# A two-layer gated cross-attention kernel: the split of the row maxima moves from VectorE to GpSimd

## The chip, the core and the metric

The kernel runs on one core of one Trainium2 chip. The metric is the device time of one execution in microseconds (us), of which the median of three runs is taken. A core has TensorE (matrix products), VectorE, ScalarE and GpSimd (elementwise work), each with its own queue that runs in order; they wait for one another by semaphores. SyncE's queue issues most of the transfers.

## The reference

Four batches of 512 rows with 128 channels pass two layers, each a gated cross-attention and a gated feed-forward part:

```python
x = x + tanh(g_xattn[0]) * attention0(layernorm(x), ctx, ctx)     # 16 heads of 8, 154 keys
x = x + tanh(g_ffn[0])   * quantised_mlp(layernorm(x))
x = x + tanh(g_xattn[1]) * attention1(layernorm(x), ctx, ctx)     # causal mask
x = x + tanh(g_ffn[1])   * gated_scan(layernorm(x))               # a recurrence over the four batches
# attention: softmax(q k^T / sqrt(8)) v, then a linear layer
```

The softmax needs the maximum of each row of scores to stay in range.

## The kernel before

**Row maxima first.** For each layer and batch (`n = 4 * layer + batch`) the kernel computes the scores twice. In the first pass TensorE (`scores_for_top`) writes scores with the 512 queries across partitions, some three heads at a time, to the three banks `ps_top`, and VectorE (`take_top`, L1333) reduces each to the negated row maximum in `nm`, 4 tiles of queries by 16 heads, so 64 numbers in each of 128 partitions. `split_top` makes two parts of type fp32r of `nm` in the tile `nms`: a high part, which is `nm` copied to fp32r (L1344), and a low part, `nm` less the high part (L1346). `turn_top` on TensorE (L967) transposes them into `ps_misc`, `copy_top` on ScalarE (L763) copies that to `nmT`, and two transfers on SyncE's queue (`tops`, L446) lay it as two more rows under the queries in `Q4`. In the second pass (`scores`, L985 and L991) each product so gives the score with its maximum taken off; ScalarE (`exps`, L772) takes the exponential, and TensorE (`weigh`, L1017) multiplies it with the values.

**The order of work.** Each engine's instructions stand in an order written out by hand. A loop runs over the layer, over `i` from -1 to 4, and over 20 slots. In iteration `i` the second pass of batch `i` (20 tiles, one a slot), the first pass of batch `i + 1` (slots 0 to 12), and the end of batch `i - 1` (division, output product, residual, statistics of the next norm) run side by side. `PE_PLAN`, `ACT_PLAN` and `DVE_PLAN` say at which slot the other pieces stand: VectorE's split of batch `i + 1` at slot 13, `turn_top` and `copy_top` at slot 14, the statistics for the norm `post` of batch `i - 1` at slot 9 and its transposes at slot 16 (18 in layer 1). The first reductions of batch `i + 2` stand in slots 17 to 19, behind `turn_top` in TensorE's order, and write `nm` again.

**GpSimd's order** has no slots. In an iteration it runs, in this order: the norm `pre` of a later batch, its block-diagonal keys (`diagonal`, L521) and the low part of its queries (`q_low`, L614), for `i` = -1 and 1 only; in layer 1 the causal masks `past(i, 0)` to `past(i, 2)` (L620), each of which waits for four exponentials, the third for that of tile 11; the norm `post` of batch `i - 1` (`normed`: L626, the power L628, L636 and four instructions `xn` of L643); in layer 1 `past(i, 3)`, which waits for tile 15; and `biased(i + 1)` (four additions, L604), which `residual` needs in the next iteration. `biased(0, 0)` stands at the end of iteration -1.

Of the kernel before, what the change touches and what calls it, by code (L numbers as in the profile page):

```python
# [7 lines left out]
F32 = mybir.dt.float32  # L8
# [3 lines left out]
ALU = mybir.AluOpType  # L12
# [4 lines left out]
B, T, C = 4, 512, 128  # L17
# [3 lines left out]
G, J = 4, 4  # L21
# [68 lines left out]
def units_before(n):  # L90

    return sum(len(UNITS[m // B]) for m in range(n))
# [109 lines left out]
def program(nc, x, w, wkr, ctxT, tailT, wffn, cols, rows, consts, masks, out):  # L202
    with ExitStack() as ctx:
        def sb(name, shape, dt=F32):
            return ctx.enter_context(nc.sbuf_tensor("sb_" + name, shape, dt))
# [4 lines left out]
        def sem(name):  # L210
            return ctx.enter_context(nc.semaphore(name))
# [44 lines left out]
        nm = sb("nm", [P, TT, H])  # L256
        nms = sb("nms", [P, TT, 2, J, G], F32R)
# [91 lines left out]
        top_r, top_red = sem("top_r"), sem("top_red")  # L349
        nmh_r, nms_r, nmT_r = sem("nmh_r"), sem("nms_r"), sem("nmT_r")  # L350
# [117 lines left out]
        def _(pool):  # L468
# [17 lines left out]
            def clear_rest():  # L486

                pool.wait_ge(kd0_r, 1)
                pool.memset(Q4[2][:, :, :].bitcast(F32), 0.0).then_inc(q4_clear, 1)
                pool.memset(Kd[2][:, :, :, :].bitcast(F32), 0.0).then_inc(kd_clear, 1)  # L490
                pool.memset(nil[:, :], 0.0).then_inc(nil_r, 1)
# [49 lines left out]
            def biases():  # L541

                pool.wait_ge(rows_in, 16)
                pool.wait_ge(gates, 1)
                for n in range(2):
                    pool.tensor_scalar(bvt[:, n, :], rows_sb[:, RV + n, :], own[:, 0:1], 1.0, ALU.mult, ALU.mult)\
                        .then_inc(bias_r, 1)
                for n in range(2):
                    pool.tensor_scalar(bog[:, n, :], rows_sb[:, RO + n, :], tg[:, n:n + 1], 1.0, ALU.mult, ALU.mult)\
                        .then_inc(bias_r, 1)  # L550

            def frames():

                pool.memset(KT[:, :, :, :].bitcast(F32), 0.0).then_inc(zero_r, 1)
                pool.wait_ge(zero_r, 3)
                pool.wait_ge(ones_r, 1)
                pool.wait_ge(small_in, 32)
                pool.wait_ge(rows_in, 16)
                for j in range(J):
                    c = 16 * (j % 2) + D  # L560
                    for b in range(B):
                        ins = pool.memset(V4[:, b, :, j, c:c + D], 1.0)
                    link(ins)
                    q = slice(32 * j, 32 * j + 32)
                    on = ones[q, :].rearrange("p (b g d) -> p b g d", b=B, g=G)
                    link(pool.tensor_scalar(VT[q, :, :, 16 * j + D:16 * j + 2 * D], on, own[q, 0:1], 1.0,
                                            ALU.mult, ALU.mult))
# [26 lines left out]
            def biased(layer, b):  # L594
                n = B * layer + b
                if n >= 2:
                    pool.wait_ge(res_r, n - 1)
                if layer == 1:
                    pool.wait_ge(x2_r, b + 1)
                else:  # L600
                    pool.wait_ge(x_in[b], 16)
                pool.wait_ge(bias_r, 4)
                for t in range(TT):
                    ins = pool.tensor_tensor(xg[:, n % 2, t, :], xr[:, TT * b + t, :], bog[:, layer, :], ALU.add)  # L604
                ins.then_inc(xg_r, 1)

            def q_low(layer, b):

                n = B * layer + b
                pool.wait_ge(qh_r, n + 1)  # L610
                pool.wait_ge(qf_r, QLOW_ON_POOL.index((layer, b)) + 1)
                if n >= 2:
                    pool.wait_ge(*q_landed(n - 2))
                pool.tensor_tensor(ql[:, n % 2, :], qf[:, :], qh[:, n % 2, :].bitcast(F32), ALU.subtract).then_inc(ql_r, 1)  # L614

            def past(b, r):

                k = TILES * (B + b) + 4 * r
                pool.wait_ge(exp_r, k + 4)
                pool.affine_select(pr[:, k % PRING:k % PRING + 4, 0:P], pr[:, k % PRING:k % PRING + 4, 0:P],  # L620
                                   [[0, 4], [1, P]], ALU.is_ge, 0.0, base=0, channel_multiplier=-1).then_inc(past_r, 1)

            def root(k):

                pool.wait_ge(mv_r, k + 1)
                pool.tensor_scalar(var[:, k % 4, :], mv[:, k % 4, :, 1], EPS, 1.0, ALU.add, ALU.mult).then_inc(var_r, 1)  # L626
                pool.wait_ge(var_r, k + 1)
                pool.tensor_tensor(rstd[:, k % 4, :], var[:, k % 4, :], half[:, :], ALU.pow).then_inc(rstd_r, 1)  # L628

            def normed(kind, layer, b):  # L630

                k = norm_no[kind, layer, b]
                root(k)
                if (kind, layer, b) in NORM_ON_DVE:
                    return
                pool.tensor_scalar(nmean[:, k % 4, :], mv[:, k % 4, :, 0], -1.0, 1.0, ALU.mult, ALU.mult).then_inc(nmean_r, 1)  # L636
                nmeans[0] += 1
                pool.wait_ge(nmean_r, nmeans[0])
                pool.wait_ge(rstd_r, k + 1)
                if B * layer + b > 0:  # L640
                    pool.wait_ge(xnT_r, norm_no[kind, (B * layer + b - 1) // B, (b - 1) % B] + 1)
                for t in range(TT):
                    ins = pool.tensor_scalar(xn[:, kind == "post", t, :], xr[:, TT * b + t, :], nmean[:, k % 4, t:t + 1],  # L643
                                             rstd[:, k % 4, t:t + 1], ALU.add, ALU.mult)
                ins.then_inc(xn_r, 1)
# [3 lines left out]
            for layer in range(2):  # L649
                normed("pre", layer, 0)  # L650
                if layer == 0:
                    pool.wait_ge(xn_r, 1)
                    pool.memset(Kd[1][:, :, :, :].bitcast(F32), 0.0).then_inc(kd_clear, 1)
                    pool.memset(V4[:, :, :, :, :], 0.0).then_inc(zero_r, 1)
                    pool.memset(VT[:, :, :, :], 0.0).then_inc(zero_r, 1)
                normed("pre", layer, 1)
                if layer == 0:
                    clear_rest()
                    normed("pre", 0, 2)
                    frames()  # L660
                    biases()
                    values(0)
                    q_low(0, 2)
                    tail_keys(0)
                else:
                    clear_late()
                for i in range(-1, B + 1):
                    masked = layer == 1 and 0 <= i < B
                    if i == -1 or 0 < i < B - 2:
                        b = max(i, 0) + 2  # L670
                        if i > 0:
                            normed("pre", layer, b)
                        if masked:
                            past(i, 0)
                        diagonal(layer, b)
                        if (layer, b) != (0, 2):
                            q_low(layer, b)
                    elif masked:
                        past(i, 0)
                    if masked:  # L680
                        past(i, 1)
                        past(i, 2)
                    if 0 <= i - 1 < B:
                        normed("post", layer, i - 1)
                    if masked:
                        past(i, 3)
                    if 0 <= i + 1 < B:
                        biased(layer, i + 1)
                if layer == 0:
                    pool.wait_ge(xq_r, B)  # L690
                    diagonal(1, 0)
                    values(1)
                    tail_keys(1)
                    clear_early()
# [530 lines left out]
        def _(dve):  # L1225
# [109 lines left out]
                                  AX.X, ALU.max, negate=True).then_inc(top_red, 1)  # L1335

            def split_top(layer, b):
                n = B * layer + b
                dve.wait_ge(top_red, units_before(n + 1))
                src = nm[:, :, :].rearrange("p t (g j) -> p t j g", g=G)  # L1340
                part = [nms[:, :, a, :, :] for a in range(2)]
                if n > 0:
                    dve.wait_ge(nmT_r, n)
                dve.tensor_copy(part[0], src).then_inc(nmh_r, 1)  # L1344
                dve.wait_ge(nmh_r, n + 1)
                dve.tensor_tensor(part[1], src, part[0].bitcast(F32), ALU.subtract).then_inc(nms_r, 1)  # L1346
# [337 lines left out]
```

## Time and profile before

| | |
|---|---|
| runs | 343.42, 342.97, 343.03 us, median 343.03 |
| profiled execution, first to last instruction (span) | 341.2 us; its own time isn't listed apart from the three runs |
| TensorE busy | 279.0 us |
| VectorE busy | 252.5 us |
| ScalarE busy | 192.6 us |
| GpSimd busy | 136.7 us |
| the 8 splits on VectorE | median 0.316 + 0.326 us each |

The profile is of one execution. PE is TensorE, DVE VectorE, ACT ScalarE, POOL GpSimd, SP SyncE; L967 is line 967 of the kernel. The end of a matmul is modelled. The number behind x counts the instructions of a group.

### The profile page before, as it was taken

The page shows a single profiled execution, that of the slowest core. Times are in us where ns is not written, and L with a number is a line of the kernel's source. Part 1 is how long each engine was busy: PE and PEld are TensorE (multiplying, and loading weights), DVE is VectorE, ACT ScalarE, POOL GpSimd, SP SyncE. Part 2 cuts the span into 40 slices and gives each one's busy share as a digit, 9 for nine tenths or more (in the row PEclk, how much of TensorE's full clock was granted, in tenths as well). Part 3 has the DMA queues.
Part 4 walks back from the last instruction along what each step waited for, and adds up shares of the span by engine and source line. Part 5 has one row for each costly group of instructions (what it writes and reads, how often), then busy time and mean ns, then how long its engine had stood idle before and what let it go on. Part 6 is the DMA issues. An engine that isn't in the chain of part 4 may idle for free. (4 is left out here: it accounts for less than half of the span.)

```text
span 341.2 us, 4468 instructions
## 1 busy us (share of the span) xinstructions
PE 279.0 (82%) x1424; PEld 160.7 (47%) x1424; DVE 252.5 (74%) x538; ACT 192.6 (56%) x303; POOL 136.7 (40%) x274
## 2 busy tenths in 40 slices
PE   0889899899989779985007888899998998999994
PEld 0558544455434345331005776664654654444462
DVE  5699875877996388889989977986596693441834
ACT  1673367556476746779589632446656446665232
POOL 6669893750050411870002059921386207131100
PEclk9999999999999999997556999999999999999998
DMA  7930100010000000000000002220001000000004
GB/s 204 336 146 3 69 32 10 27 73 10 1 8 3 0 0 2 1 0 0 1 0 0 2 0 92 94 100 2 10 25 76 8 0 10 1 0 3 0 1 123
DMA packets 9687, 12.55 MB, mean 37 GB/s; under 512 B 896, under 2 KB 5376, under 8 KB 9664
## 3 DMA queue, kind: packets, MB, share of 16 engines
q1 hardware_dynamic: 9232, 11.80, 9.7%
q10 hardware_dynamic: 432, 0.47, 0.7%
q8 instruction: 11, 0.18, 0.2%
q14 instruction: 12, 0.10, 0.1%
HBM read 4.27 MB, written 1.05 MB: 16 GB/s over the span
## 5 line engine op out<-in xcount | busy, mean ns | idle before, releaser
L1333 DVE TENSOR_REDUCE sb_nm<-ps_top 128x3 f32<-128x462 f32 (+2 forms) x168 | 96.0, 626 | 26.6 <-PE ps_top L953 13.9
L772 ACT ACTIVATE sb_pr<-ps_score 128x512 f32<-128x512 f32 (+1 forms) x148 | 82.3, 583 | 58.8 <-PE ps_score L985 49.2
L953 PE MATMUL ps_top<-sb_Kd,sb_Q 128*128 128x462 f32 (+3 forms) x240 | 69.7, 349 | 4.7 <-DVE sb_nm L1333 2.4
L985 PE MATMUL ps_score<-sb_Q,sb_Kd 128*128 128x512 f32 x119 | 54.4, 467 | 1.3 <-ACT sb_pr L772 1.0
L953 PEld LDWEIGHTS ps_top<-sb_Kd,sb_Q 128*128 128x128 f32 x240 | 42.6, 188 | 18.1 <-DVE sb_nm L1333 11.9
L626 POOL TENSOR_SCALAR sb_var<-sb_mv 128x4 f32<-128x4 f32 x16 | 4.7, 291 | 83.3 <-DVE sb_mv L1296 82.9
L985 PEld LDWEIGHTS ps_score<-sb_Q,sb_Kd 128*128 128x128 f32 x119 | 22.2, 188 | 31.6 <-ACT sb_pr L772 23.4
L1017 PE MATMUL ps_pv<-sb_pr,sb_V 128*32 128x512 f32 x256 | 34.1, 605 | 0.0
L620 POOL TENSOR_SCALAR_AFFINE_SELECT sb_pr<-sb_pr 128x512 f32<-128x512 f32 x16 | 10.6, 661 | 46.4 <-ACT sb_pr L772 46.4
L1353 DVE STREAM_TRANSPOSE sb_oq<-ps_pv 128x512 f32<-128x512 f32 x16 | 10.8, 700 | 12.4 <-PE ps_pv L1017 12.3
L643 POOL TENSOR_SCALAR sb_xn<-sb_xr,sb_nmean,sb_rstd 128x128 f32<-128x128 f32 x44 | 19.3, 453 | 1.2
L628 POOL TENSOR_TENSOR sb_rstd<-sb_var,sb_half 128x4 f32<-128x4 f32 x16 | 17.7, 1106 | 1.3
L521 POOL CAST sb_Kd<-sb_K 32x616 fp32r<-32x616 f32 x20 | 14.1, 703 | 8.5 <-DVE sb_K L1244 7.4
L1017 PE MATMUL ps_pv<-sb_pr,sb_VT 128*32 128x512 f32 (+1 forms) x128 | 14.9, 550 | 0.9 <-ACT sb_pr L772 0.9
L1102 PE MATMUL ps_top<-sb_wfT 128*128 128x256 f32 x30 | 9.5, 472 | 7.2 <-DVE sb_amax L1470 6.4
L991 PE MATMUL ps_score<-sb_Q,sb_KT 128*128 128x384 f32 (+1 forms) x29 | 12.9, 454 | 2.7 <-ACT sb_pr L772 2.7
L1293 DVE BATCH_NORM_STATS2 sb_stat<-sb_xr 128x6 f32<-128x128 f32 x64 | 13.9, 280 | 1.4 <-DMA sb_xr<-x 1.2
L497 POOL MEMSET sb_Q<- 128x2048 f32 x1 | 1.8, 1804 | 32.6 <-DVE sb_amax L1470 32.6
L930 PE MATMUL ps_misc<-sb_consts,sb_xn 128*128 128x128 f32 x64 | 10.4, 287 | 5.1 <-POOL sb_xn L643 2.3
L1195 PE MATMUL ps_top<-sb_front,sb_wfT 128*128 128x512 f32 x22 | 12.1, 682 | 2.7 <-ACT sb_uf L830 2.2
L1084 PE MATMUL ps_misc<-sb_consts,sb_amx 128*128 128x128 f32 x8 | 2.5, 400 | 14.2 <-DVE sb_amx L1403 14.2
L604 POOL TENSOR_TENSOR sb_xg<-sb_xr,sb_bog 128x128 f32<-128x128 f32 x32 | 13.6, 457 | 0.1
(180 smaller groups left out, 556.5 us busy)
## 6 DMA issues: line engine op xcount, KB each, us to landing
sb_Q<-sb_qh SPq DMA_DIRECT2D x16, 256.0 KB, 2.3
sb_Q<-sb_ql SPq DMA_DIRECT2D x8, 256.0 KB, 3.3
sb_xr<-x SPq DMA_DIRECT2D x4, 256.0 KB, 7.7
out<-sb_xr SPq DMA_DIRECT2D x4, 256.0 KB, 2.5
sb_wsb<-w SPq DMA_DIRECT2D x1, 704.0 KB, 9.0
sb_wf<-wffn SPq DMA_DIRECT2D x1, 576.0 KB, 8.6
sb_wkr<-wkr SPq DMA_DIRECT2D x2, 256.0 KB, 7.1
sb_Q<-sb_nmT SPq DMA_DIRECT2D x16, 32.0 KB
```

The lines of the kernel that those rows point to most:

```text
L521: ins = pool.tensor_copy(Kd[n % 3][q, :, j, :], K4[q, :, b, :])
L604: ins = pool.tensor_tensor(xg[:, n % 2, t, :], xr[:, TT * b + t, :], bog[:, layer, :], ALU.add)
L628: pool.tensor_tensor(rstd[:, k % 4, :], var[:, k % 4, :], half[:, :], ALU.pow).then_inc(rstd_r, 1)
L643: ins = pool.tensor_scalar(xn[:, kind == "post", t, :], xr[:, TT * b + t, :], nmean[:, k % 4, t:t + 1], rstd[:, k % 4, t:t + 1], ALU.add, ...
L772: act.activation(pr[:, k % PRING, q0:T], score_bank(B * layer + b, t)[:, q0:T], ACT.Exp, scale=SCALE).then_inc(exp_r, 1)
L953: ins = pe.matmul(cols[:, c0:c1, :], Q4[n % 3][:, g, P * qt:P * qt + P], Kd[n % 3][:, g, j:j + c1 - c0, 0:keys], start=True, stop=not mask ...
L985: ins = pe.matmul(ps[:, :], Kd[n % 3][:, g, j, 0:P], Q4[n % 3][:, g, :], start=True, stop=True, skip_group_check=True)
L991: ins = pe.matmul(ps[:, q0:T], KT[:, b, t - H, :], Q4[n % 3][:, t - H, q0:T], start=True, stop=(layer == 0), skip_group_check=True)
L1017: ins = pe.matmul(acc[32 * g:32 * g + 32, q0:T], lhs, pr[:, (TILES * n + t) % PRING, q0:T], start=(r in (0, 2)), stop=(r >= 4), skip_group ...
L1195: pe.matmul(fbank[t % FRING][:, :], wfT[:, 3 * (t // 12) + m, :], xq[:, c, :], start=True, stop=True).then_inc(fmm, 1)
L1293: ins = dve.bn_stats(stat6[:, k % 4, t, :], xr[:, TT * b + t, :])
L1333: dve.tensor_reduce(nm[:, :, :].rearrange("p t h -> p (t h)")[:, f0:f0 + heads], top[k % MRING][:, 0:keys * heads].rearrange("p (h k) -> p ...
```

## The change

The two instructions of `split_top` for batches 1, 2 and 3 of each layer run on GpSimd; VectorE keeps batch 0 of each layer. The semaphores stay the same. On GpSimd the call stands behind `normed("post", layer, i - 1)` and ahead of `past(i, 3)` and `biased(layer, i + 1)`.

```diff
+            def split_top(layer, b):
+
+                n = B * layer + b
+                pool.wait_ge(top_red, units_before(n + 1))
+                src = nm[:, :, :].rearrange("p t (g j) -> p t j g", g=G)
+                part = [nms[:, :, a, :, :] for a in range(2)]
+                pool.wait_ge(nmT_r, n)
+                pool.tensor_copy(part[0], src).then_inc(nmh_r, 1)
+                pool.wait_ge(nmh_r, n + 1)
+                pool.tensor_tensor(part[1], src, part[0].bitcast(F32), ALU.subtract).then_inc(nms_r, 1)
+
...
                     if 0 <= i - 1 < B:
                         normed("post", layer, i - 1)
+                    if 0 < i + 1 < B:
+                        split_top(layer, i + 1)
                     if masked:
                         past(i, 3)
                     if 0 <= i + 1 < B:
...
             def split_top(layer, b):
+                if b > 0:
+                    return
                 n = B * layer + b
                 dve.wait_ge(top_red, units_before(n + 1))
```

## Rows read from the trace of the kernel before

**Rows 1.** The page: busy time of each engine; granted clock in 40 slices
```profile
PE 279.0 (82%) x1424; PEld 160.7 (47%) x1424; DVE 252.5 (74%) x538; ACT 192.6 (56%) x303; POOL 136.7 (40%) x274
...
PEclk9999999999999999997556999999999999999998
```
**Rows 2.** The tile `nms`: duration in ns (min/median/max), first and last start
```profile
L1344 DVE CAST sb_nms<-sb_nm x8: 217/316/664, 34.7 to 284.2; 128x64 fp32r<-128x64 f32 x8
L1346 DVE TENSOR_TENSOR sb_nms<-sb_nm,sb_nms x8: 264/326/409, 35.0 to 284.5; 128x64 fp32r<-128x64 f32 x8
```
**Rows 3.** Timeline, layer 0, batch 1: start us, duration us, engine, line
```profile
49.70 3.36 POOL L604 TENSOR_TENSOR sb_xg<-sb_xr,sb_bog 128x128 f32<-128x128 f32 x8
50.68 0.38 DVE L1346 TENSOR_TENSOR sb_nms<-sb_nm,sb_nms 128x64 fp32r<-128x64 f32 x1
51.12 0.61 PE L967 MATMUL ps_misc<-sb_consts,sb_nms 128*32 128x128 f32 x4
```
**Rows 4.** Timeline, layer 0, batch 2
```profile
74.17 0.41 DVE L1346 TENSOR_TENSOR sb_nms<-sb_nm,sb_nms 128x64 fp32r<-128x64 f32 x1
74.63 0.61 PE L967 MATMUL ps_misc<-sb_consts,sb_nms 128*32 128x128 f32 x4
74.89 1.71 POOL L604 TENSOR_TENSOR sb_xg<-sb_xr,sb_bog 128x128 f32<-128x128 f32 x4
```
**Rows 5.** Timeline, layer 1, batch 1
```profile
236.43 0.64 POOL L620 TENSOR_SCALAR_AFFINE_SELECT sb_pr<-sb_pr 128x512 f32<-128x512 f32 x1 [3.86 <-ACT sb_pr L772]
237.44 0.27 DVE L1346 TENSOR_TENSOR sb_nms<-sb_nm,sb_nms 128x64 fp32r<-128x64 f32 x1
238.32 0.61 PE L967 MATMUL ps_misc<-sb_consts,sb_nms 128*32 128x128 f32 x4
```
**Rows 6.** Timeline, layer 1, batch 2; in brackets idle time before, and its releaser
```profile
259.28 0.64 POOL L620 TENSOR_SCALAR_AFFINE_SELECT sb_pr<-sb_pr 128x512 f32<-128x512 f32 x1 [2.56 <-ACT sb_pr L772]
...
260.29 1.03 POOL L628 TENSOR_TENSOR sb_rstd<-sb_var,sb_half 128x4 f32<-128x4 f32 x1
261.40 0.19 POOL L636 TENSOR_SCALAR sb_nmean<-sb_mv 128x4 f32<-128x4 f32 x1
...
261.54 0.26 DVE L1346 TENSOR_TENSOR sb_nms<-sb_nm,sb_nms 128x64 fp32r<-128x64 f32 x1
261.70 1.75 POOL L643 TENSOR_SCALAR sb_xn<-sb_xr,sb_nmean,sb_rstd 128x128 f32<-128x128 f32 x4
...
261.86 0.61 PE L967 MATMUL ps_misc<-sb_consts,sb_nms 128*32 128x128 f32 x4 [0.25 <-DVE sb_nms L1346]
...
264.68 1.44 DVE L1333 TENSOR_REDUCE sb_nm<-ps_top 128x4 f32<-128x512 f32 x2 [2.88 <-PE ps_top L957]
```
**Rows 7.** GpSimd: two groups by shape (busy us, mean ns), one line (min/median/max)
```profile
L604 POOL TENSOR_TENSOR sb_xg<-sb_xr,sb_bog 128x128 f32<-128x128 f32 x32 | 13.6, 457 | 0.1
L614 POOL TENSOR_TENSOR sb_ql<-sb_qf,sb_qh 128x512 fp32r<-128x512 f32 x4 | 5.1, 1277 | 3.3 <-ACT sb_qf L755 3.1
L534 POOL CAST sb_KT<-sb_K x8: 601/612/1232, 43.9 to 151.2; 32x512 fp32r<-32x512 f32 x8
```
**Rows 8.** TensorE's timeline; then stretches of 1 us, PEclk third from last
```profile
154.57 3.62 PE L1195 MATMUL ps_top<-sb_front,sb_wfT 128*128 128x512 f32 x4 [2.22 <-ACT sb_uf L830]
158.52 1.13 PE L1195 MATMUL ps_pv<-sb_front,sb_wfT 128*128 128x512 f32 x2 [0.33 <-ACT sb_uf L830]
...
222.06 0.61 PE L967 MATMUL ps_misc<-sb_consts,sb_nms 128*32 128x128 f32 x4 [1.57 <-DVE sb_nms L1346]
...
154.00:155.00 1.00, 0.43 (x1) 0.35 (x2) 1.00 (x1) 1.00 (x4) 0.00 (x0) 0.88 0.00 0
155.00:156.00 1.00, 1.00 (x2) 0.34 (x1) 1.00 (x2) 1.00 (x2) 0.00 (x0) 0.50 0.00 0
...
158.00:159.00 1.00, 0.67 (x2) 0.30 (x2) 0.96 (x2) 1.00 (x3) 0.00 (x0) 0.91 0.00 0
...
161.00:162.00 1.00, 0.00 (x0) 0.00 (x0) 1.00 (x3) 1.00 (x3) 0.00 (x0) 0.80 0.00 0
```

## The prediction

> **What bounds the kernel now.** I read the page's busy times first [rows 1]: TensorE is busy 82% of the span, VectorE 74%, GpSimd 40%. The average says that GpSimd has room for more; it doesn't say whether the room is where the split stands. So next the view of the tile that holds the two parts [rows 2]: eight CASTs and eight subtractions on VectorE, 0.32 and 0.33 us by the median. Who needs them is TensorE alone: `turn_top` stands in its queue right behind the scores of slot 14 and waits for `nms_r`; behind it in the same queue are the scores of tiles 15 to 19, and behind `copy_top` on ScalarE are their exponentials. So the question at each batch is one comparison of times: when do the parts land, and when does TensorE come to them? For that I read the timeline around each of the six splits that move [rows 3 to 6], with GpSimd's queue beside it.
>
> In layer 0 TensorE starts the four transposes 0.05 to 0.06 us after VectorE's subtraction ends: at 51.12 us after 51.06 [rows 3], at 74.63 after 74.58 [rows 4]. TensorE is waiting for the parts there already, by a little. In layer 1 the transposes start at 261.86 after 261.80, with TensorE idle 0.25 us before them [rows 6]. Only for batch 1 of layer 1 do they start well behind the parts, at 238.32 after 237.71 [rows 5]: TensorE had the weighing of round 2 to finish. So at five of six places the split ends the wait of the engine that has the most work, and any lateness is passed on whole.
>
> **The change, part by part.** What goes: six CASTs and six subtractions on VectorE. Worth nothing, I find: behind the split VectorE has nothing that could start sooner. In layer 1 its next reduction waits until 264.68, 2.88 us idle, for scores that TensorE issues behind the transposes [rows 6]; in layer 0 the next is the maximum of the normed rows, which waits for GpSimd's `xn`. That is the cover; without it six splits of 0.64 us would be 3.9 us [rows 2].
>
> What comes: the same two instructions on GpSimd, 64 elements in each of 128 partitions, with a wait between them. The trace has no such instruction there, so I work from its neighbours. A subtraction or addition took 457 ns at 128 elements and 1277 ns at 512 [rows 7]: 2.14 ns for one more element, so 0.32 us at 64. A CAST took 612 ns at 512 elements by the median [rows 7], and the instruction with 4 elements that writes `nmean` 0.19 to 0.20 us [rows 6]: 0.81 ns for one more, so 0.25 us at 64. The hand-over of one GpSimd instruction's result to the next is 0.08 us (261.32 to 261.40) [rows 6]. Together 0.65 us. From below each instruction costs at least those 0.20 us, so 0.48 for the split; from above each costs at most the 457 ns of one with 128 elements and two tensors, so 0.99. I take 0.65, since 64 elements lie between these sizes, and keep 0.48 and 0.99 for the range. From the end of the subtraction to TensorE's start I add the 0.05 us that VectorE's takes.
>
> The size of the instruction is the lesser part. The greater is where the split stands in GpSimd's queue, which runs in order: behind `normed("post", layer, i - 1)` and, in layer 1, behind `past(i, 2)`.
>
> Layer 0, batch 1: in front of it stands `biased(0, 0)`, the first four of the eight additions that begin at 49.70 [rows 3]; the row shows no idle time ahead of them, so the engine is not free earlier. Four take 1.7 us [rows 4], and the next instruction starts at 51.38. Parts at 52.03, TensorE at 52.08 in place of 51.12: 0.96 late. What moves behind the split is `biased(0, 1)`, which nobody needs before the residual of the next iteration.
>
> Layer 0, batch 2: `normed("post", 0, 0)` holds GpSimd until its next instruction starts at 74.89 [rows 4]. Parts at 75.54, TensorE at 75.59 in place of 74.63: 0.96 late. Batch 3 repeats this row by row (0.96 too). So 2.9 us for layer 0.
>
> Layer 1, batch 1: no `post` yet. GpSimd is idle after `past(0, 2)` ends at 237.07, and VectorE's split began some 0.25 us ahead of 237.44 [rows 5]. The parts would land at about 237.9, or at 238.2 by the upper bound, and TensorE comes at 238.32. No cost; the cover is 0.4 us.
>
> Layer 1, batch 2: `past(1, 2)` starts at 259.28, since it waits for the exponentials of tile 11; only then come the root, the mean and four `xn` of `normed("post", 1, 0)`, from 260.0 to 263.45 [rows 6]. The split starts at 263.40, as consecutive instructions overlap by 0.05. Parts at 264.05, TensorE at 264.10 in place of 261.86: 2.24 late. Batch 3 repeats it, again 2.24. So 4.5 us for layer 1. `past(i, 3)` and `biased(i + 1)` are now behind the split, but they wait for exponentials that come later by the same 2.24, so they cost nothing more.
>
> Stalls: 3 x 0.96 + 0 + 2 x 2.24 = 7.4 us. All later work of the iteration, on ScalarE, VectorE and the queue of the two DMAs of `nmT`, starts from these transposes, and I find no wait of TensorE behind them that ends on something that isn't late as well. So nothing is given back.
>
> **The clock.** The two stalls of layer 1 are longer than they look: TensorE already idles 0.25 us there, so each is a gap of 2.5 us. The trace has one gap of 2.22 us, before 154.57; the granted clock then fell from full (2.4 GHz) to half (1.2 GHz) at about 154.8 and was back at about 158.2, and the four matmuls in it took 3.62 us, 0.9 each. It fell a second time at about 161.6, when TensorE had been idle since 159.65. A gap of 1.57 us, before 222.06, brought no fall: the line of the page with the granted clock in 40 slices of 8.5 us shows full speed there [rows 1, 8]. So gaps like those of layer 0 (about 1 us) are safe, and each of the two in layer 1 may bring a fall. At half clock from 154.8 to 158.2, 3.4 us of matmul time do 1.7 us of work; after the transposes TensorE still has one short wait, so I take 1.6 us for a fall. The trace has two falls for gaps of this size and none for smaller ones, but the clock fell 2.4 us after TensorE's stop in one and 2.0 us after it in the other, so the length of the gap isn't all that decides, so I give each gap a chance of 0.55: none falls 0.2, one 0.5, both 0.3. One fall is the likeliest: +1.6.
>
> Sum: the median of the runs is 343.0, 1.8 above the profiled span of 341.2, and I add to the median as the parts around the span don't change. 343.0 + 7.4 + 1.6 = 352.0 us.
>
> No row has a GpSimd instruction that reads every fourth word, as both of these do; the bounds above stand in for it. The Trainium skill ("GPSIMD Engine Reference", section Performance pitfalls for Q7 kernels) says that reads whose step is above 8 bytes take about 2.9 cycles an element in place of 1.9; by it, an estimate, each of the two instructions would be some 0.05 us longer, and the sum 352.5.
>
> **The rivals.**
> Both gaps bring a fall: 352.0 + 1.6 = 353.6. For it: both falls on record follow idle stretches of about 2 us. Neither brings one: 350.4. For it: both gaps on record lie in a stretch where TensorE has little to do anyway, and here it is busy on both sides.
>
> The split is dear: the strided reads bring it to the upper bound, 0.34 us more at five places, 1.7 us: 353.7 with one fall. Against it: the sizes from 128 to 512 lie near one line. The page's pitfall above is this mechanism in a smaller size.
>
> Part is given back: TensorE's later waits for VectorE's reductions and for ScalarE shrink, because those engines have caught up in the stall. At half of the 7.4 us, and no fall, 346.7. Against it: both are idle behind each split, so there is no backlog to catch up with.
>
> Faster: the relieved VectorE is what sets the pace, and the parts come in time because GpSimd gets through `post` before VectorE's last reduction. Then the 3.9 us of [rows 2] come off: 339.1. It decides from the point where GpSimd comes free ahead of VectorE's own split, whose subtractions start at 74.17 and 261.54 [rows 4, 6]; it is free at 74.9 and 263.4.
>
> **How the numbers follow.** One fall 0.40, both 0.22, none 0.17, a dear split 0.11, part given back 0.06, faster 0.02, no difference (within 0.2%, about what a measurement of this kernel can tell from no change) 0.02. The range takes in the first four, 0.90 of the chance: from 350.4 less the five splits at the lower bound (0.17 x 5 = 0.9, so 349.5; I stop at 349.8) to 353.7 and a little of the dear split with both falls: 354.2. Slower by over 0.2%: 0.96.
>
> **What would show it.** In the profile after: the waits of `ps_misc` L967 for `nms` name GpSimd, and are some 1 us in layer 0 and 2.5 us twice in layer 1; the transposes of batch 1 of layer 1 start without a wait; GpSimd's CAST 0.25 and subtraction 0.32 us, started within 0.1 us behind the last `xn` or `xg`; the span is equal to before up to 50 us and then late in steps of 0.96, 0.96, 0.96, 0, 2.24 and 2.24; the granted clock below 1.00 for some 3 us behind one of the last two. The forecast is wrong if GpSimd's first instruction waits for something that I didn't see, if later waits shrink so that the steps don't stay, or if a split takes over 1 us.

## The result, and the profile after

The changed kernel takes 356.25 us (median; 352.96 to 357.34) against 343.06 us (342.97 to 343.42) for the kernel before on the same chip: a ratio of 1.036, interval 1.033 to 1.039, so slower, by 13.2 us between the medians. The forecast was 352.0 with a range up to 354.2: the sign is right, the time lies outside the range. The profiled execution took 355.27 us with a span of 353.2; its counterpart of before had a span of 341.2, 12.0 us less.

The page of the changed kernel, busy times and the granted clock in 40 slices, answers to [rows 1]:
```profile
PE 282.1 (80%) x1424; PEld 162.2 (46%) x1424; DVE 249.1 (71%) x526; ACT 192.9 (55%) x303; POOL 139.9 (40%) x286
...
PEclk9999999999999999998558999999999996799999
```
VectorE has been relieved, and the span is longer all the same. The clock line has the dip of before between the layers (slices from 159 to 194 us, in the kernel before from 154 to 188), and a new one in two slices late in layer 1, at 291 to 309 us.

The view of the tile with the two parts answers to [rows 2] (min, median, max in ns; first and last start):
```profile
L623 POOL CAST sb_nms<-sb_nm x6: 287/287/292, 51.8 to 292.1; 128x64 fp32r<-128x64 f32 x6
L625 POOL TENSOR_TENSOR sb_nms<-sb_nm,sb_nms x6: 340/342/346, 52.2 to 292.5; 128x64 fp32r<-128x64 f32 x6
L1359 DVE CAST sb_nms<-sb_nm x2: 271/454/637, 35.3 to 224.4; 128x64 fp32r<-128x64 f32 x2
```
The waits, summed by engine and line (us in total, times, longest):
```profile
PEld ps_misc L980 <- POOL sb_nms L625: 11.8, 6, 3.5
...
PE ps_misc L980 <- POOL sb_nms L625: 8.2, 5, 2.6
```
TensorE now waits for GpSimd's parts five times of six, 8.2 us together. The timeline shows each; line 980 is line 967 of before (answers to [rows 3 to 6]):
```profile
52.59 0.61 PE L980 MATMUL ps_misc<-sb_consts,sb_nms 128*32 128x128 f32 x4 [0.89 <-POOL sb_nms L625]
...
241.81 0.61 PE L980 MATMUL ps_misc<-sb_consts,sb_nms 128*32 128x128 f32 x4
...
292.85 0.61 PE L980 MATMUL ps_misc<-sb_consts,sb_nms 128*32 128x128 f32 x4 [2.55 <-POOL sb_nms L625]
```
Batches 2 and 3 of layer 0 wait 1.09 us each (at 77.09 and 99.96), batch 2 of layer 1 waits 2.55 (at 267.62), as the last row does; batch 1 of layer 1 (the middle row) waits for nothing. Why 2.55, GpSimd's own timeline tells:
```profile
262.75 0.63 POOL L631 TENSOR_SCALAR_AFFINE_SELECT sb_pr<-sb_pr 128x512 f32<-128x512 f32 x1 [2.58 <-ACT sb_pr L785]
263.47 0.20 POOL L637 TENSOR_SCALAR sb_var<-sb_mv 128x4 f32<-128x4 f32 x1
263.75 1.03 POOL L639 TENSOR_TENSOR sb_rstd<-sb_var,sb_half 128x4 f32<-128x4 f32 x1
264.87 0.19 POOL L647 TENSOR_SCALAR sb_nmean<-sb_mv 128x4 f32<-128x4 f32 x1
265.17 1.74 POOL L654 TENSOR_SCALAR sb_xn<-sb_xr,sb_nmean,sb_rstd 128x128 f32<-128x128 f32 x4
266.85 0.29 POOL L623 CAST sb_nms<-sb_nm 128x64 fp32r<-128x64 f32 x1
267.23 0.34 POOL L625 TENSOR_TENSOR sb_nms<-sb_nm,sb_nms 128x64 fp32r<-128x64 f32 x1
```
From 262.75 on the engine waits for nothing: the split takes 0.7 us, and 4.1 us of other work stand ahead of it in the queue.

Where do the 12.0 us come in? I compare starts of the same instructions in both traces. GpSimd's `xg` of 49.70 [rows 3] starts at 50.19, 0.5 us later before any split has run. That is scatter and not the change: in the second trace of the same program, further down, the same stretch is 0.2 us earlier than before. Then the lateness grows by 1.0, 1.0, 1.0, 0, 2.3 and 2.3 at the six splits. That makes 8.1 with the 0.5. The rest arises behind the last one. Two rows of TensorE's timeline of the kernel before:
```profile
284.80 0.61 PE L967 MATMUL ps_misc<-sb_consts,sb_nms 128*32 128x128 f32 x4 [0.25 <-DVE sb_nms L1346]
...
292.51 0.50 PE L985 MATMUL ps_score<-sb_Q,sb_Kd 128*128 128x512 f32 x1
```
The changed kernel has the same two at 292.85 (above) and here:
```profile
296.73 1.94 PE L1030 MATMUL ps_pv<-sb_pr,sb_V 128*32 128x512 f32 x8
...
304.52 0.50 PE L998 MATMUL ps_score<-sb_Q,sb_Kd 128*128 128x512 f32 x1
```
8.05 us late has become 12.01. The eight matmuls of L1030 take 1.94 us where they took 1.06. Stretches of the changed kernel (length; busy us of PE, PEld, DVE, ACT, POOL; granted clock third from last):
```profile
293.00:294.00 1.00, 0.88 (x7) 0.65 (x5) 0.00 (x0) 0.50 (x2) 0.00 (x0) 1.00 0.07 16
294.00:295.00 1.00, 0.39 (x1) 0.39 (x2) 0.00 (x0) 0.94 (x3) 0.37 (x1) 0.55 0.00 0
...
295.00:304.00 9.00, 9.00 (x38) 3.62 (x37) 0.72 (x1) 4.35 (x8) 1.93 (x5) 0.50 0.02 8
...
304.00:305.00 1.00, 1.00 (x10) 0.44 (x3) 0.33 (x1) 0.00 (x0) 0.64 (x1) 0.83 0.00 0
```
The clock was at half (1.2 GHz) from about 294.1 to 304.3 us, 10.2 us in which TensorE was busy almost throughout. I had assumed 3.4. The lateness grows there though no wait is longer than before; everywhere else it stays level between the splits. Behind the other gap of 2.55 us the clock did not fall in this execution.

### The profile page after: what moved, and what is told of

Same layout as the page of the kernel before. It is cut to its first block and busy times, and to the rows that moved or that the text cites. A ratio compares the mean times of both kernels' runs of the same rounds, so it can differ in the third digit from the quotient of the medians.

```text
span 353.2 us, 4468 instructions
## 1 busy us (share of the span) xinstructions
PE 282.1 (80%) x1424; PEld 162.2 (46%) x1424; DVE 249.1 (71%) x526; ACT 192.9 (55%) x303; POOL 139.9 (40%) x286
## 5 line engine op out<-in xcount | busy, mean ns | idle before, releaser
L998 PE MATMUL ps_score<-sb_Q,sb_Kd 128*128 128x512 f32 x119 | 55.4, 476 | 1.1 <-ACT sb_pr L785 0.8
L1030 PE MATMUL ps_pv<-sb_pr,sb_V 128*32 128x512 f32 x256 | 35.0, 619 | 0.0
L1030 PE MATMUL ps_pv<-sb_pr,sb_VT 128*32 128x512 f32 (+1 forms) x128 | 16.1, 590 | 0.9 <-ACT sb_pr L785 0.9
L776 ACT ACTIVATE sb_nmT<-ps_misc 32x512 fp32r<-32x512 f32 x8 | 4.7, 587 | 15.9 <-PE ps_misc L980 15.9
```

The lines of the kernel that those rows point to most:

```text
L998: ins = pe.matmul(ps[:, :], Kd[n % 3][:, g, j, 0:P], Q4[n % 3][:, g, :], start=True, stop=True, skip_group_check=True)
L1030: ins = pe.matmul(acc[32 * g:32 * g + 32, q0:T], lhs, pr[:, (TILES * n + t) % PRING, q0:T], start=(r in (0, 2)), stop=(r >= 4), skip_group ...
```

## The experiments

Theory: the extra time is five stalls (7.4 us), plus falls of the clock behind the two long gaps, which cost more than I gave them. Rivals: GpSimd's split or something else it does is dearer than the stalls show; or the time is lost to an effect of GpSimd's share in the work that isn't lateness. Medians of the kernel before were 343.14, 343.18 and 343.19 us in the three groups of runs.

**One layer alone.** Two kernels in which GpSimd splits only in layer 0, or only in layer 1 (VectorE does the rest):
```
-                    if 0 < i + 1 < B:
+                    if layer == 0 and 0 < i + 1 < B:      # layer == 1 in the other
                         split_top(layer, i + 1)
...
-                if b > 0:                                 # VectorE's split_top
+                if layer == 0 and b > 0:
                     return
```


> Only layer 0's batches 1 to 3 are split on GpSimd, layer 1 stays on VectorE. If the cost is the lateness of the parts, handed on whole: three stalls of 0.96 to 1.03 us, 343.1 + 3.0 = 346.1 us, runs within 0.5 us of one another, the granted clock as before, since gaps of about 1 us bring no fall. If the cost came from GpSimd and VectorE holding each other up, VectorE's own rows in 50 to 100 us would be longer and the time above 346.5. If TensorE made up for the stalls, below 345.

> Only layer 1's batches 1 to 3 are split on GpSimd. Lateness alone: 0 + 2.3 + 2.3, 343.1 + 4.6 = 347.7 us. With the clock: some 4 us more for each of the two gaps behind which it falls, so runs between 347.7 and 355.7 that differ by steps of some us, with a lower mean clock where the time is longer, and a median of 351 to 353. If the scatter of the changed kernel had another cause than these two gaps, the runs would agree at 347.7.

Layer 0 alone: 346.20 us (346.02 to 346.31), ratio 1.0088 [1.0075, 1.0101]; 3.06 more than before against 2.9 forecast. In its trace the lateness grows by 0.9, 1.0 and 1.0 us at the three splits and stays level between them, so GpSimd and VectorE don't hold each other up. Layer 1 alone: 351.25 us, ratio 1.0236 [1.0205, 1.0267], its six runs between 349.03 and 353.21. So layer 0 is closed, and both the excess and the scatter are layer 1's. Its profiled run was its fastest, 349.03 us, with two waits of 2.54 and 2.55 us and one fall:
```profile
266.00:268.00 2.00, 2.00 (x8) 1.72 (x7) 0.69 (x1) 0.98 (x2) 1.97 (x5) 0.51 0.12 41
268.00:270.00 2.00, 2.00 (x14) 0.92 (x12) 0.69 (x1) 0.60 (x1) 0.00 (x0) 0.64 0.00 0
270.00:272.00 2.00, 2.00 (x12) 1.46 (x9) 0.62 (x1) 0.88 (x2) 0.00 (x0) 1.00 0.00 0
```
Here the half clock lasted some 3.4 us and cost 1.5, just as the forecast has it. That is the cheapest case, not the usual one.

**The gaps filled.** The changed kernel, with five matmuls on data already there, whose result nobody reads, in the two long gaps (each is two instructions in the profile, so x10). They start once VectorE's reductions are done, so they fill the wait for GpSimd and don't shorten it:
```
             def turn_top(layer, b):
                 n = B * layer + b
+                if layer == 1 and b >= 2:
+                    pe.wait_ge(top_red, units_before(n + 1))
+                    keep_warm(5)
                 pe.wait_ge(nms_r, n + 1)
```


> The changed kernel, and in layer 1 TensorE runs five matmuls that nobody reads while it waits for the parts of batches 2 and 3; the parts come no earlier. If the falls of the clock come from TensorE standing idle there: no fall, 343.1 + 7.6 = 350.7 us, runs within 1 us, the clock in the profile at full between 230 us and the end. If the clock fell for another reason: 355 to 357 as the changed kernel.

350.83 us (350.72 to 352.24), ratio 1.0232 [1.0217, 1.0248]. TensorE's timeline, and the clock over all of layer 1:
```profile
264.43 2.43 PE L1118 MATMUL ps_top<-sb_wfT 128*128 128x256 f32 x10
267.05 0.61 PE L983 MATMUL ps_misc<-sb_consts,sb_nms 128*32 128x128 f32 x4 [0.19 <-POOL sb_nms L625]
```
```profile
230.00:348.00 118.00, 108.36 (x565) 59.20 (x564) 65.92 (x144) 59.93 (x107) 35.75 (x69) 1.00 0.06 21
```
The transposes come late by the same steps as in the changed kernel (they stand 0.57 us earlier, at 267.05 for 267.62, because this execution lacks the 0.5 us from ahead of the first split), the clock stays full, and 5.4 of the 13.2 us are gone. The trace ends 7.5 us later than before, all of it from the six steps. This separates the two terms: stalls 350.83 - 343.14 = 7.7 us (7.4 forecast), falls 356.25 - 350.83 = 5.4 us (1.6 forecast); by the second set of runs of the changed kernel, further down, 355.52 - 350.83 = 4.7. One of the four runs was at 352.24; it has no trace.

**Is GpSimd's own time on the path?** The same kernel as the last, with the CAST on GpSimd done twice:
```
+                link(pool.tensor_copy(part[0], src))
                 pool.tensor_copy(part[0], src).then_inc(nmh_r, 1)
```


> The kernel with the filled gaps, and GpSimd does each CAST twice. If the time of GpSimd's two instructions lies on the path at five of six places: 5 x 0.37 = 1.9 us more than with the filled gaps alone, 352.7 us. If it is hidden, 350.8.

352.57 us (352.09 to 352.88): 1.7 more than the run with filled gaps. The second CAST puts the subtraction off by 0.35 us (starts of the two CASTs in GpSimd's timeline), five times 1.75:
```profile
267.53 0.29 POOL L623 CAST sb_nms<-sb_nm 128x64 fp32r<-128x64 f32 x1
267.88 0.29 POOL L624 CAST sb_nms<-sb_nm 128x64 fp32r<-128x64 f32 x1
268.26 0.34 POOL L626 TENSOR_TENSOR sb_nms<-sb_nm,sb_nms 128x64 fp32r<-128x64 f32 x1
```
In this trace the lateness grows by 1.3, 1.35, 1.35, 0, 2.65 and 2.65. So the delay is passed on whole at five places and not at the sixth.

**Late parts without GpSimd.** The kernel before, in which VectorE fills an unused tile four times, or three times, ahead of its splits of batches 2 and 3 of layer 1:
```
+                if layer == 1 and b >= 2:
+                    for _ in range(LATE):                 # 4; 3 in the second kernel
+                        link(dve.memset(gap1[:, :], 0.0))
                 dve.tensor_copy(part[0], src).then_inc(nmh_r, 1)
```


> The kernel before with all splits on VectorE, but in layer 1, ahead of the splits of batches 2 and 3, VectorE clears a tile that nobody reads, four times, some 0.6 us each. If only the lateness of the parts counts, whichever engine makes them: 343.1 + 2 x 2.4 = 347.9 us without a fall of the clock, and the same falls and scatter as with layer 1 alone on GpSimd, so a median of 350 to 353. If GpSimd's taking part were the cause: 347.9 or less, without scatter.

> As the late VectorE before it, with three clearings in place of four. With four, of 0.56 us and 0.19 us of waiting each, the parts were 3.05 us late; with three they are 2.3 us late, as GpSimd's are in layer 1 of the changed kernel. If which engine makes them late doesn't matter: the time of layer 1 alone on GpSimd, 351.3 us by the median and 349 to 353.5 by run, 343.1 + 4.6 = 347.7 where the clock doesn't fall. If GpSimd adds something of its own: 1 us or more below that.

With four, 354.42 us (353.69 to 354.77), ratio 1.0324 [1.0309, 1.0339], above the 350 to 353 expected. I had sized each fill at 0.6 us; it took 0.56, and 0.19 more to the next, so the parts came 3.05 us late, not 2.4: 6.1 us of stalls, and 354.42 - 343.18 - 6.1 = 5.1 for the falls, of which its trace has two of 6.8 us. That is why it was repeated with three. Then 352.47 us (350.16 to 354.13), ratio 1.0277 [1.0248, 1.0307], which overlaps that of layer 1 on GpSimd, 1.0236 [1.0205, 1.0267]. The gap is the same:
```profile
264.06 0.61 PE L968 MATMUL ps_misc<-sb_consts,sb_nms 128*32 128x128 f32 x4 [2.52 <-DVE sb_nms L1350]
```
4.5 us of the 9.3 are the stalls (2 x (2.52 - 0.25)) and 4.8 the falls; its trace, of a run of 354.1 us, has a fall behind each gap, of 6.8 and 10.2 us. Which engine is late makes no difference that these runs can tell: the rival that GpSimd does harm beyond its lateness falls.

**The changed kernel once more**, unchanged, for a second trace.

> The changed kernel again, for the scatter of its runs and where the clock falls in another profile. If its time is 350.7 us (the stalls) and a fall of the clock behind zero, one or two gaps: runs from 351 to 358, the longer the lower their mean clock, median 354 to 357. If the first runs were an odd draw: the runs agree within 1 us.

355.52 us (353.71 to 357.45), ratio 1.0366 [1.0333, 1.0398]. This trace has a fall behind both gaps, half clock for some 6.8 us each, and 2.8 and 2.1 us lost, 4.9 together. Stretches around the first:
```profile
266.00:268.00 2.00, 1.04 (x7) 0.80 (x7) 0.00 (x0) 0.53 (x2) 0.69 (x3) 0.96 0.00 0
268.00:270.00 2.00, 1.41 (x4) 1.31 (x5) 0.00 (x0) 1.41 (x4) 1.39 (x3) 0.50 0.07 27
...
274.00:276.00 2.00, 2.00 (x11) 1.43 (x8) 0.44 (x1) 0.69 (x2) 0.00 (x0) 0.83 0.00 0
```
Of the ten runs of the changed kernel the lowest is 352.96, 2.1 above the kernel with filled gaps. Four had a mean clock of 0.950 to 0.951 and took 352.96 to 355.27 us; six had 0.932 to 0.937 and took 355.43 to 357.45. The trace with one fall is of the first group, that with two of the second. It would be wrong to count falls by this. A stretch between the layers and layer 1 itself, first in the trace with one fall, then in this one:
```profile
150.00:200.00 50.00, 23.51 (x94) 15.23 (x93) 47.47 (x66) 41.14 (x35) 6.88 (x8) 0.76 0.00 0
230.00:348.00 118.00, 107.56 (x547) 57.59 (x547) 64.43 (x143) 58.99 (x105) 35.74 (x69) 0.96 0.04 14
...
150.00:200.00 50.00, 25.88 (x99) 16.48 (x98) 47.47 (x66) 41.14 (x35) 6.90 (x8) 0.69 0.00 0
230.00:348.00 118.00, 107.94 (x543) 58.30 (x542) 63.47 (x141) 58.68 (x105) 35.72 (x69) 0.94 0.03 11
```
Most of the difference in mean clock comes from between the layers (about 23.9 us at half clock in one, 30.7 in the other), where the lateness doesn't change in either trace. In layer 1 they differ by 3.4 us only, since the one fall was of 10.2 and the two of 6.8. How many falls the other eight runs had isn't known.

**The split ahead of the norm.** Layer 1 alone, on GpSimd, but ahead of `post` in its queue:
```
+                    if layer == 1 and 0 < i + 1 < B:
+                        split_top(layer, i + 1)
                     if 0 <= i - 1 < B:
                         normed("post", layer, i - 1)
-                    if 0 < i + 1 < B:
-                        split_top(layer, i + 1)
```


> Layer 0 split on VectorE as before; in layer 1 GpSimd does the split ahead of the norm of the batch before, not behind it. If the place in GpSimd's queue made the 2.24 us: the parts are late only by what GpSimd's two instructions and hand-over take longer than VectorE's, 0.2 to 0.3 us for batches 2 and 3 and 0 for batch 1, so 343.1 + 0.5 = 343.6 us and no fall. If GpSimd as such is the cost, wherever the split stands: 347.7 us or more.

345.72 us (344.75 to 347.63), ratio 1.0074 [1.0051, 1.0097], 2.1 more than expected. What moving it brings is there: 5.5 us less than with the split behind `post`. But the norm is now the one that waits:
```profile
285.40 0.61 PE L980 MATMUL ps_misc<-sb_consts,sb_nms 128*32 128x128 f32 x4 [0.49 <-POOL sb_nms L625]
...
287.17 0.44 PE L1004 MATMUL ps_score<-sb_Q,sb_KT 128*128 128x384 f32 x1 [0.73 <-ACT sb_pr L785]
...
288.92 0.66 PE L943 MATMUL ps_misc<-sb_consts,sb_xn 128*128 128x128 f32 x4 [0.92 <-POOL sb_xn L654]
```
```profile
290.00:292.00 2.00, 2.00 (x11) 0.82 (x3) 0.00 (x0) 0.36 (x2) 1.12 (x3) 0.50 0.00 0
```
Three gaps of under 1 us each, within 4 us, and the clock went to half behind them, for some 6.8 us and a loss of 2.8 us in this trace (1.67 us late at 288.92, 4.4 at the counterpart of 292.51). That trace is of the slowest of the six runs, 347.63 us; no run fills these gaps, so that they brought the fall is argued from the order in time. So neither of the two places tried in GpSimd's queue is free in layer 1.

**The consumer moved instead.** The transposes and their copy two slots later in the plans of TensorE and ScalarE, in the changed kernel; and one slot later in the kernel before:
```
-           (14, "top", 1)      # PE_PLAN and ACT_PLAN
+           (16, "top", 1)      # changed kernel; (15, "top", 1) in the kernel before
```


> The changed kernel with the transposes of the parts, and their copy on ScalarE, two slots later (16 in place of 14), so that TensorE does the scores of tiles 15 and 16 first. If the cost is TensorE standing behind the parts: of each stall some 0.8 us are filled, so about 0.2 left in layer 0 and 1.4 in layer 1, 343.1 + 3.5 = 346.6 us, with fewer falls of the clock. If the chain from the parts over ScalarE and the two transfers to the next batch's scores is what counts: no gain, or a wait of those scores for the transfers, 350 us and more.

> The kernel before with transposes and copy one slot later (15). TensorE waits 0.05 to 0.28 us for VectorE's parts at five places; a score ahead of them would fill that: 342.3 to 343.0 us. If the chain over ScalarE and the transfers counts, later transposes cost: 343.5 us or more.

In the changed kernel: 349.95 us (349.66 to 350.67), ratio 1.0200 [1.0185, 1.0214]; better than 356.25, but 3.4 short of what was expected. In layer 0 the transposes wait for nothing now, but what needs their result does, and in layer 1 the gap shrinks only to 1.95:
```profile
76.68 0.63 PE L943 MATMUL ps_misc<-sb_consts,sb_xn 128*128 128x128 f32 x4 [0.77 <-ACT sb_nmT L776]
...
265.92 0.92 PE L980 MATMUL ps_misc<-sb_consts,sb_nms 128*32 128x128 f32 x4 [1.95 <-POOL sb_nms L625]
```
The four transposes take 0.92 us in place of 0.61: the half clock is there too, and so it is behind the second gap, of 1.91 us, for some 3.4 us each time.

In the kernel before: 341.42 us (340.80 to 342.29), ratio 0.9949 [0.9933, 0.9965]. It is the fastest of all that ran, and faster than the 342.3 to 343.0 expected. In batch 2 of layer 1 the 0.25 us ahead of the transposes [rows 6] are gone, and also the 0.73 us that TensorE waited for ScalarE behind them; some score of another tile now stands in each place:
```profile
261.35 0.60 PE L967 MATMUL ps_misc<-sb_consts,sb_nms 128*32 128x128 f32 x4
261.70 0.44 PE L991 MATMUL ps_score<-sb_Q,sb_KT 128*128 128x384 f32 x1
...
262.20 0.44 PE L991 MATMUL ps_score<-sb_Q,sb_KT 128*128 128x384 f32 x1
```
Not all of these 0.98 us is gained: the starts behind them are 0.8 us earlier than in the kernel before. Batches 1 and 3 of layer 1 add 0.5 each, and what layer 0 gains on the way is gone again at its end. That makes 1.8, as the spans (339.4 for 341.2) and the medians have it. My expectation counted only the waits ahead of the transposes; the larger part is the wait for ScalarE behind them.

## Why the prediction was wrong, point by point

**The place where it is decided** was right: TensorE's wait for the parts at five of six splits, none at batch 1 of layer 1, and nothing given back later (the lateness of each step stays to the end). That VectorE gains nothing from the relief also holds: its busy time shrinks and the span doesn't.

**The price of the split**, 0.65 us, was 0.71 (51.82 to 52.53 in GpSimd's timeline): CAST 0.29 for 0.25, subtraction 0.34 for 0.32, hand-over 0.08 as read. Well inside the bounds. The Trainium skill ("GPSIMD Engine Reference", Performance pitfalls for Q7 kernels) would have each some 0.05 us longer for its strided read, by an estimate from its cycles per element; the rows show 0.04 and 0.02 over my interpolation, which has that sign. No run here reads the same elements packed, so the cause isn't shown.

**The stalls**, 7.4 us by 3 x 0.96 and 2 x 2.24, measured 7.7 (filled gaps), from steps of 1.0, 1.0, 1.0, 0, 2.3 and 2.3. This part was right by its mechanism and not by luck: each step came where it was forecast, within 0.1 us.

**The clock** is the term that failed. The step was "I take 1.6 us for a fall", which rests on falls that last 3.4 us as the one before 158.2 did [rows 8], and "one fall is the likeliest". Measured: half clock for 3.4, 6.8, 6.8 and 10.2 us in the traces of the changed kernel and of layer 1 alone, at a cost of 1.5 us for the shortest, 2.8 and 2.1 for the two of 6.8, and 4.0 for the longest; 5.4 us in all by the medians where the sum has 1.6. I had read the length off a single fall. The same rows had a second, and I gave only its start, 161.6: it lasted 23.9 us, to 185.5. Two rows of the kernel before, inside it and at its end:
```profile
175.00:180.00 5.00, 0.00 (x0) 0.00 (x0) 4.43 (x9) 4.29 (x3) 0.00 (x0) 0.50 0.00 0
...
185.00:190.00 5.00, 4.15 (x18) 2.97 (x16) 4.83 (x7) 5.00 (x4) 1.22 (x1) 0.95 0.00 0
```
TensorE had little to do there, so it is no measure of a fall in layer 1, but it shows that 3.4 us was not the only length on record. The number of falls was too low as well: I gave each gap 0.55. Of the eight gaps of 2.52 to 2.55 us in four traces (the changed kernel twice, layer 1 alone, VectorE late with three fills), six had a fall: one of 3.4 us, three of 6.8 and two of 10.2. That is 1.5 falls a run for my 1.1, at 2.8 us on average (1.5 to 4.0) for my 1.6: 4.2 us a run, where the medians say 4.7 to 5.4. The rival "both gaps bring a fall" names the case of one of the two traces of the changed kernel, a run of 355.43 us, and priced it at 353.6, with the same 1.6.

**The other rivals**: a dear split is refuted by its duration; part given back, by the filled gaps (7.7, not 3.7); faster, by the waits, for the reason given there: GpSimd comes free behind VectorE's own split.

What stays open is what sets how long the half clock lasts, how many falls the runs without a trace had, and why the first gap of 2.55 us had no fall in one trace and one in another of the same program.

## What to carry to other kernels

Work on the path moved to a less busy engine costs what stands ahead of it in that engine's in-order queue: here 0.7 us of work came up to 2.3 us late, against an engine that is idle 60% of the time. A gap put into TensorE's queue has two prices, its length and what the clock does behind it; the second scatters from run to run, so give it a range from several falls, not the length of one, and read every fall that the trace has to its end. A mean clock over the whole run doesn't count the falls that cost time: it also holds those in stretches where TensorE isn't on the path. Where a consumer waits for its data by a little, try the consumer one slot later first: it gained 0.5% here, while moving the producer's work to another engine lost 3.6%.

## What the runs showed of the hardware

The granted clock fell to half behind six of eight gaps of 2.52 to 2.55 us on a TensorE that was otherwise busy, and behind two of 1.95 and 1.91 us in one trace; it did not fall behind one of 1.57 us [rows 8]. It stayed at half for 3.4 to 10.2 us behind gaps of the same 2.5 us, though TensorE was busy throughout (9.00 us busy in 9.00 us at 0.50). Each us at half clock in layer 1 cost 0.31 to 0.45 us of time. At least one reason that it isn't 0.5 shows: a wait for ScalarE of 0.73 us shrank to 0.38 in the second fall of the second trace. Three gaps of 0.49, 0.73 and 0.92 us within 4 us were followed by a fall, in the one trace of that kernel. Ten matmul instructions on unused data, 2.4 us, in each of the two gaps kept the clock at 1.00 through all of layer 1 in the profiled run, and were worth 4.7 to 5.4 us.
